# Projecting rotary queries and keys with both rotary halves in one bank, from weight rows regrouped on chip

## The reference, cut to what matters

```
xn = layernorm(x)                                   # x: 32 samples x 256 tokens x 128
Q, K, V = einsum('bsm,qhdm->bqhsd', xn, W_qkv)      # 16 heads of 64
Q, K = [first 32 columns * cos + rotate_half(first 32) * sin, last 32 columns as they are]
attn = softmax(causal(Q K^T) / 8) V ;  a = attn W_o
f = top-2 of 8 experts (+ a skip gate) over xn, gelu MLP of 512
out = x + a + f
```

## Time and profile before

| what | value |
|---|---|
| median of 3 runs | 1582.79 us (1578.91 to 1585.89) |
| span of the profiled execution | 1643.9 us |
| PE busy in the span | 1341.7 us, 82% |
| ACT, DVE, POOL busy | 71%, 70%, 60% |
| start of the sample loop's steps, about | 102 us |
| end of the sample loop, about | 1230 us |

### The profile page before, as it was taken

One profiled execution on the slowest core, in us unless ns is written; L12 is line 12 of the kernel. 1 busy time (PEld: TensorE's weight loads), 2 busy tenths in 40 slices (PEclk: granted clock), 3 DMA queues, 4 the chain that ended last, 5 costly groups with the idle time before them and its releaser, 6 DMA issues.

```text
span 1643.9 us, 48543 instructions
## 1 busy us (share of the span) xinstructions
PE 1341.7 (82%) x13156; PEld 1038.9 (63%) x13157; DVE 1143.8 (70%) x4325; ACT 1174.3 (71%) x3758; POOL 987.4 (60%) x1697
## 2 busy tenths in 40 slices
PE   2529999999999999999999999999977999576620
PEld 1417766777666776766777667766656988455520
DVE  6788776777777777767777777777756777354531
ACT  7409887888888888878888878888877888334310
POOL 3208777777777787777777777776760000454555
PEclk9859999999999999999999999999998999788865
DMA  9623544334553335543345433355423333222242
GB/s 302 164 49 83 115 115 102 86 84 97 115 119 87 86 84 109 120 104 86 85 93 117 117 91 85 84 110 117 105 89 94 87 85 85 72 77 77 79 129 64
DMA packets 125894, 166.49 MB, mean 101 GB/s; under 512 B 15504, under 2 KB 85392, under 8 KB 125456
## 3 DMA queue, kind: packets, MB, share of 16 engines
q1 hardware_dynamic: 117296, 147.50, 37.6%
q0 software_dynamic: 8416, 17.33, 3.6%
HBM read 30.42 MB, written 33.69 MB: 39 GB/s over the span
## 4 chain that ended last, share of the span: by engine, by line
POOL 30%; issue 20%; PE 18%; DMA 16%; DVE 7%; another core or an unknown queue 3%; ACT 2%; DVEq 1%; POOLq 1%; SPq 1%; ACTq 0%
DMA sorted_x_dram<-send_x,send_at 15%; POOL probs L433 8%; POOL probs L432 7%; POOL arena L417 7%; PE bank L1034 4%; PE bank L1033 4%; PE bank L1035 4%; POOL arena L422 4%; POOL sorted_x_dram L437 3%; PE bank L1132 1%; PE bank L1166 1%; PE bank L1118 1%; DVE arena L690 1%; POOL arena L482 1%
## 5 line engine op out<-in xcount | busy, mean ns | idle before, releaser
L577 ACT ACTIVATE probs<-arena,neg_max 128x128 f32<-128x128 f32 (+1 forms) x1024 | 455.4, 448 | 126.5 <-DVE neg_max L887 112.1
L432 POOL TENSOR_TENSOR probs<-probs,inv_total 128x128 f32<-128x128 f32 x512 | 208.2, 407 | 247.8 <-DMA sorted_x_dram<-send_x,send_at 126.4
L1118 PE MATMUL bank<-ident,probs 128*128 128x128 f32 x1536 | 263.2, 280 | 70.6 <-POOL probs L433 62.6
L887 DVE CUSTOM_DVE_ANT_0 arena<-bank,causal 128x128 f32<-128x128 f32 (+1 forms) x1024 | 314.9, 345 | 0.0
L482 POOL DMA_INDIRECT arena<-sorted_y_dram,slots x128 | 123.7, 967 | 273.6 <-DMA sorted_y_dram<-arena 171.6
L1118 PEld LDWEIGHTS bank<-ident,probs 128*128 128x128 f32 x1536 | 173.6, 141 | 144.9 <-issue 87.9
L894 DVE RECIPROCAL inv_total<-total 128x2 f32<-128x2 f32 x512 | 82.9, 162 | 254.4 <-PE bank L1109 178.1
L433 POOL TENSOR_SCALAR probs<-probs,inv_total 128x256 f32<-128x256 f32 x512 | 251.4, 491 | 0.0
L417 POOL TENSOR_TENSOR arena<-arena 128x256 f32<-128x256 f32 x256 | 189.8, 752 | 64.0 <-DVE arena L849 58.8
L1033 PE MATMUL bank<-xnT_lo,wqk_hi 128*128 (+1 forms) x768 | 212.2, 276 | 10.7 <-DVE arena L855 10.2
L1035 PE MATMUL bank<-xnT_hi,wqk_hi 128*128 (+1 forms) x768 | 212.1, 276 | 0.0
(11 more groups left out here) (158 smaller groups left out, 3675.6 us busy)
## 6 DMA issues: line engine op xcount, KB each, us to landing
second<-arena SPq DMA_DIRECT2D x128, 256.0 KB, 4.2
arena<-arena SPq DMA_DIRECT2D x128, 256.0 KB, 4.1
second<-arena SPq DMA_DIRECT2D x128, 128.0 KB
arena<-arena SPq DMA_DIRECT2D x128, 128.0 KB
arena<-sorted_x_dram SPq DMA_DIRECT2D x80, 128.0 KB
sorted_y_dram<-arena SPq DMA_DIRECT2D x80, 128.0 KB
sorted_x_dram<-arena SPq DMA_DIRECT2D x3, 2560.0 KB, 21.2
arena<-experts_dram SPq DMA_DIRECT2D x8, 512.0 KB, 4.5
```

What stands on the lines that cost most here:

```text
L432: nc.gpsimd.tensor_tensor(p0, p0, inv_total[:, s % 4, 0:1].broadcast_to([P, P]), ALU.mult)
L577: last = nc.scalar.activation(probs[:, s % 4, at:at + w], masked[:, s % 2, at:at + w], ACT.Exp, bias=neg_max[:, s % 2, t:t + 1], scale=-1. ...
L887: last = nc.vector.tensor_tensor_reduce(out=masked[:, s % 2, at:at + w], in0=SC[s % 2][:, at:at + w], in1=causal[:, at:at + w], scale=1.0, ...
L1118: last = nc.tensor.transpose(TP[s % 2][:, k * P:(k + 1) * P], probs[:, s % 4, k * P:(k + 1) * P], ident[:])
```

## The change

Half rows. The 16 rotary columns x1 of eight heads make one group of 128 rows, and the x2 of the same eight heads another. A rope unit now holds x1 in its first 256 columns and x2 in its second, for eight heads. `turn` multiplies the whole bank once by cos and once by sin (two instructions), and `rope_add` computes x1 cos - x2 sin and x2 cos + x1 sin (two instructions). The swapped groups are gone: 16 groups instead of 24, 4 rope units a sample instead of 8. The rows are picked out of the loaded weights by strided reads when they are split into high and low (32 small instructions in place of 2 large ones). Float16 staging of rotary columns is by half and eight heads, so the stacking of each group of four heads needs 5 transfers for q and 5 for k: one of the plain columns (32 partitions to 64) and four of rotary columns, each from 16 partitions to 32. That is 40 a sample instead of 16, with the same bytes. The table `BESIDE`, the projection banks (2 instead of 3) and the banks of attend's output (2 instead of 1) change too, and so do buffers of the rotation (one pair of products instead of two buffers, two sums instead of four).

```diff
-    [("rest", 0)], [("rest", 1), ("rope", 0)], [("rope", 1)], [("rope", 2), ("rope", 3)],
-    [("rest", 2)], [("rest", 3), ("rope", 4)], [], [("rope", 5), ("rope", 6)],
-    [("rope", 7)], [("v_high", 0), ("v_high", 1)], [], [("y", 0)],
-    [("v_low", 0)], [("y", 1)], [("v_low", 1)], [],
+    [("rest", 0)], [("rope", 0)], [("rest", 1)], [("rope", 1)],
+    [("rest", 2)], [("rope", 2)], [("rest", 3)], [("rope", 3)],
+    [("v_high", 0)], [], [("v_high", 1)], [("y", 0)],
+    [("y", 1)], [("v_low", 0)], [("v_low", 1)], [],
 ]
-PJ_BANKS = 3
+PJ_BANKS = 2
...
+        def rope_rows(u, c):
+            g = 8 * (u // 2) + 2 * (u % 2)
+            return raw_qk[:, g:g + 2, :].rearrange("p g (r n) -> p (g r) n", r=GRP)[:, :, c * 16:c * 16 + 16]
+        WQK = [(2 * u + c, rope_rows(u, c)) for u in range(ROPES) for c in range(2)]
...
             def stack_q(n, parity):
-                sp.wait_ge(q_rope_lo, 4 * n + 4)
+                sp.wait_ge(q_rope_lo, 2 * n + 2)
                 for r in range(GRP):
-                    for half_at in range(2):
-                        sp.dma_start(q_stack[parity][64 * half_at:64 * half_at + 64, r, :, :].rearrange("p l n -> p (l n)"),
-                                     q_staged[32 * r:32 * r + 32, :, :, :].rearrange("p k l n -> p (k l n)")).then_inc(q_stacked[r], 16)
+                    sp.dma_start(q_stack[parity][64:128, r, :, :, :].rearrange("p h l n -> p (h l n)"),
+                                 q_rest[32 * r:32 * r + 32, :, :, :].rearrange("p h l n -> p (h l n)").unsqueeze(1)
+                                 .broadcast_to([32, 2, 2048])).then_inc(q_stacked[r], 16)
+                    for h in range(2):
+                        for c in range(2):
+                            rows = slice(64 * h + 16 * r, 64 * h + 16 * r + 16)
+                            sp.dma_start(q_stack[parity][32 * c:32 * c + 32, r, h, :, :].rearrange("p l n -> p (l n)"),
+                                         q_rope[rows, c, :, :].rearrange("p l n -> p (l n)").unsqueeze(1)
+                                         .broadcast_to([16, 2, 1024])).then_inc(q_stacked[r], 16)
...
-                t = turned[j % 2]
-                nc.gpsimd.tensor_tensor(roped[j % 4], t[:, 0:SEQ], t[:, SEQ:2 * SEQ], ALU.add).then_inc(rope_sum, 1)
+                r = roped[j % 2]
+                nc.gpsimd.tensor_tensor(r[:, 0, :], by_cos[:, 0, :], by_sin[:, 1, :], ALU.subtract)
+                nc.gpsimd.tensor_tensor(r[:, 1, :], by_cos[:, 1, :], by_sin[:, 0, :], ALU.add).then_inc(rope_sum, 1)
...
-                nc.vector.tensor_tensor(turned[j % 2], psum[:], rot_q if j < NG else rot_k,
-                                        ALU.mult).then_inc(turn_done, 1)
+                nc.vector.tensor_tensor(by_cos, both, cos, ALU.mult)
+                nc.vector.tensor_tensor(by_sin, both, sin, ALU.mult).then_inc(turn_done, 1)
```

170 lines of the change are left out of this document (94 added, 76 removed).

## The result

The changed kernel took 1631.42 us (median of 4 runs, 1626.77 to 1635.39), the kernel before beside it 1580.85 us: ratio 1.030 (interval 1.027 to 1.034). It is 50 us slower, where I had forecast 24 us faster, and it lies above the range.

A forecast was written before the change was run, and what follows sets the result against it. PE was taken to bound steps 1 to 11, and after the change the stacking chain each sample: 31 x (33.8 - 34.7) = -28, +4 outside the loop, so -24 from 1582.8 gives 1559 us, range 1522 to 1608.

The forecast's parts named there:

- the hold of the large transfers on SP: Stacking on SP's queue: 0.2 us a sample added because large transfers still hold SP.
- the clock after the stall: PE's clock in the sample loop: taken as full speed throughout and no part of the question, so no cost.
- PE's side: Sample loop: four fewer rope units save PE 2.6 us a sample; steps 1 to 11 gain 2.1, giving 32.6 us unhindered.
- The chain decides: Loop from a sample's first scores through stacking to the next scores: sets 33.8 us a sample instead of 34.7.
- First transfer to keys landed: Stacking, from the first query transfer until the keys step 0 needs have landed: 18.3 us.
- The price of a small transfer: SP's time for each stacking transfer: 0.645 us, so 15.5 us for 24.
- the break-even: SP's queue: at 0.69 us a transfer a sample takes as long as before.
- Scores to first transfer: Steps 0 to 5, from first scores to first query transfer: 16.56 us becomes 15.5, a gain of 1.1.
- SP becomes the bound: Rival on SP's queue: dearer transfers make samples longer, 1608 us at 0.72 each, 1667 at 0.80; chance 0.25.
- Half rate by fewer source partitions: Rival in the stacking: reading 16 partitions halves the byte rate, sample 34.4 us, kernel 1578 us; chance 0.22.
- Outside the loop: Weight split and prologue rotation ahead of the loop: +4 us in all; expert part untouched.
- DVE or POOL takes PE's gain: Rival in steps 1 to 11: bunched work cuts the gain from 2.1 to 1 us; no chance of its own.

The follow-up runs named there:

- e5: Changed kernel with the four large query transfers started ahead of the wait for the last rotary low part: 1593.95 us, ratio 1.005 to the kernel before.
- e13: As e5, but from the third sample on only two of the 40 stacking transfers are made (other data): 1585.93 us, ratio 1.000 to the kernel before.
- e3: Changed kernel with stacking in the old number and shape, 8 query and 8 key transfers of 32 partitions to 64 (other data): ratio 1.010 to the kernel before.
- e4: Kernel before with only its stacking cut into 40 transfers, same bytes and data: ratio 1.046 to the uncut kernel before.
- e1: Changed kernel with the first four heads' key transfers put ahead of the last four heads' query transfers on SP's queue: ratio 1.019 to the kernel before.
- r_after: Changed kernel, unaltered, profiled once more on the same chip as the kernel before: 1630.5 us, ratio 1.029 to the kernel before.
- e9: Changed kernel with six samples in the loop's body instead of two: 1642.5 us, ratio 1.037 to the kernel before.
- e2: Changed kernel with each rotary query transfer reading 32 partitions once instead of 16 twice (other data): ratio 1.041 to the kernel before.
- r_before: Kernel before, unaltered, profiled once more on the same chip as the changed kernel: 1580.1 us (one run).
- e7: As e5, with six samples in the loop's body instead of two: 1542.3 us, ratio 0.973 to the kernel before.
- e8: Kernel before with six samples in the loop's body instead of two: 1599.5 us, ratio 1.009 to the kernel before.

## Why the prediction was wrong, point by point

In one sentence: the place and the kind of the limit were right, and two terms of its sum were too small, the hold of the large transfers on SP (0.2 us, measured 2.0) and the clock after the stall (nothing, measured 0.9 us a sample).

- **PE's side** was right in its sum: 2.6 us less work (974.65 / 30 = 32.5 us a sample before, 29.99 in e5's undisturbed sample). "A sample would take 32.6 us with nothing else in the way": 32.4 in e5, 32.5 in e13. But the working was wrong twice, and the errors cancelled, which is luck. Steps 1 to 11 gained nothing instead of 2.1 (22.5 us; the wait of 1.3 in step 10 and smaller ones took it). The steps behind them, where I "counted no change", gained 2.4 (9.5 us before, 7.1 in e5). There POOL's waits for sends went from 47.5 us to the 10.6 below in the changed kernel, and to none in e5. They come back in e3, whose transfers are large (44.4), but they also stay in e4, the kernel before with small ones (41.5). So neither the transfers nor the computing part removes them alone. The row of the changed kernel, 400 to 800 us:

```profile
POOL probs L461 <- DMA sorted_x_dram<-send_x,send_at: 10.6, 11, 1.2
```

- **The chain decides**: right in place and kind, as was the wait before step 0 for a transfer. With what e1, e5 and e13 show of it, it is shown, not argued.
- **First transfer to keys landed** is the step that failed most: 20.3 us on average in r_after instead of 18.3. The price of a small transfer, 0.645, was right (10.24 / 16 = 0.64). The term "0.2 for the large ones that still hold SP" was 2.0 (14.9 for the 20 query transfers, less 12.9): each group of four small ones behind a large one was held 0.4 to 0.7 us longer. The rest, key transfers and landing, was 5.5 for 5.2, because of the 6.1 us ahead of the samples after a jump. In my own words the break-even was 0.69 us a transfer, "only 0.05 above"; counted that way it came to (20.3 - 2.6) / 24 = 0.74.
- **Scores to first transfer**: 15.8 on average instead of 15.5. At full clock it was 14.9, better than I had thought; the 18 samples with the lower clock in step 0 take 16.4. I had left the clock out ("the clock is no part of the question") on the clock row of the kernel before, whose PE does not stall before step 0. The stall that I forecast myself (1.2 us a sample, measured 3.1) came with it: 0.9 us a sample on average.
- **What turned the sign.** The errors of 0.3 and 2.0 turned -0.9 us a sample into +1.3. With the parts of the undisturbed samples, 14.9 + 14.9 + 4.8, a sample would take 34.6 us, just below the 34.8 of before. This is an estimate from r_after's own samples, and no run tests it: the held transfers alone would have eaten the gain, and the clock and the late keys after a jump would have made the loss. e9, with fewer jumps, was no faster: its query transfers took 15.5 us instead of 14.9, for a reason that I don't know.
- **The rival "SP becomes the bound"** is what happened, with 0.25, and the range ended at its mildest form. One sum there was off as well: at 0.60 us a transfer the sample would be 1.1 us shorter and the kernel near 1525 us, not 1540.
- **Half rate by fewer source partitions**: refuted by e2. The rate fell to 143 GB/s, but the transfers are no faster when 32 partitions are read. The rule of the Trainium skill (SBUF — State Buffer, "Door 1: The DMA port swizzle"), by which I gave this 0.22, decides nothing here: SP's own 0.64 us for 64 KB is 102 GB/s, below the 109 GB/s that I had estimated from the page for 16 partitions. The two are so near that only e2 tells them apart.
- **Outside the loop** +4 us were 5.8 ahead of sample 0. e3 with 16 transfers has this loss too (its sample 0 starts at 107.5), so it isn't the stacking; the 1.8 more than forecast I did not test. Sample 0 itself, one of the 31 for which I had -0.9, lost 5.7: PE stood 5.3 us before sample 1 for its transfers, so this is the same chain. e3 has 45.1 us there, r_after 50.2, r_before 44.5. Sample 0's own longer stacking cost nothing, as I had thought.
- **DVE or POOL takes PE's gain** had "no chance of its own". True for the time of the changed kernel, since the chain was longer. But e3 shows that the change would have brought nothing even with free stacking: no gain in steps 1 to 11, the sends, and the jump (36.2 us after one, 34.3 otherwise).
- **The loop's jump** I had not thought of at all. In the changed kernel it shows only as PE's longer stall before the odd samples (3.8 us instead of 2.4), under which a stand of DVE would be hidden. With the chain cut, it costs 5.9 us at each jump. Why the kernel before hides it is argued only: its PE has 4.4 us of work in steps 0 and 1, e5's 3.7, and its DVE stands 2.2 us, not 3.9.

## What to carry to other kernels

When a stage of a pipeline feeds its own next round, add up the whole ring and ask how far each term may be off before the sign turns; here 1 us in 35 did it, and the forecast should have been nearer to even. Count transfers, not bytes, once they are small, and start each as soon as its own data is there: moving four starts ahead of a wait gave back 37 of the 44 us lost (r_after and e5 against the eight runs beside them). A stall has a second price when the engine's clock falls behind it; add it to the ring. And when a stall goes, look at samples one by one, not at their mean: e5's 35.1 us were 32.4 and 38.3, and the difference was the loop's jump.

## What the runs showed of the hardware

- SP starts a small SBUF to SBUF transfer every 0.64 us: sixteen of 64 KB from 16 partitions in 10.24 us (e5), four of 32 KB in 2.51 (after), four of 128 KB from 32 partitions in 2.58. Large ones of 256 KB took 0.91 each in a row of four (e5), and in the mixed order each held the four small ones behind it 0.4 to 0.7 us longer.
- At a jump back of a loop DVE stood 2.2 us (r_before), 3.1 (e13) and 3.9 (e5), PE not at all with two samples in the body and 3.4 to 4.2 us with six (e7, e8). Beside it the DMA record shows three to eight fetches of instructions, at other samples at most two.
- The send of step 9, an indirect transfer, landed 5.8 us after its start where sixteen stacking transfers of 128 and 256 KB ran (r_before, e3), 4.2 with the same bytes in 40 transfers in the kernel before (e4), and 2.8 and 2.9 in the changed one and e5. POOL's waits for all sends in 400 us follow this only in part: 46.7 and 44.4 us with sixteen, but 41.5 in e4, 10.4 in r_after and 0 in e5.
- In r_after 14 of 15 stalls of PE of 3.3 us or more before step 0, and 4 of 15 shorter ones (2.2 to 3.0 us), came with a stretch at 1.2 GHz in step 0; none followed the wait of 1.3 us in step 10. The length of that stall is not the whole account: in e4 29 of 30 samples have the stretch, and many of its stalls before step 0 are only 1.0 to 1.8 us.
